# Third and fourth layer steps by image: linear attention, gated mix and the expert combination issued per image in one block

## The reference

```python
# layer 0, feed-forward: one expert of 8 for each token, capacity 128 tokens an expert
x += tanh(g) * gate * (gelu(h @ w1[e]) @ w2[e])          # h = layernorm(x)
# layer 1, attention: linear attention, 16 heads of 8
q = relu((h @ Wq + bq) * 8**-0.5) + 1e-6                 # h = layernorm(x)
k = relu((ctx @ Wk + bk) * 8**-0.5) + 1e-6;  v = ctx @ Wv + bv
x += tanh(g) * ((q @ (k^T v)) / (q . sum(k) + 1e-8) @ Wo + bo)
# layer 1, feed-forward: mix with the token before
xr = mu_r * h + (1 - mu_r) * h_prev;  xk = mu_k * h + (1 - mu_k) * h_prev
x += tanh(g) * (sigmoid(xr @ W_r) * (relu(xk @ W_k)**2 @ W_v))
# layer 2, attention: softmax attention with a mask, 16 heads of 8; then routed experts
```

## Time and profile before

| | |
|---|---|
| runs (us) | 536.28, 536.67, 537.48 |
| profiled execution | 537.36 us, of which the span shown is 535.6 us |
| TensorE (PE) busy | 461.1 us, 86% |
| VectorE (DVE) busy | 293.7 us, 55% |
| ScalarE (ACT) busy | 227.7 us, 43% |
| GpSimd (POOL) busy | 91.1 us, 17% |
| chain that ended last | PE 64%, DVE 21%, ACT 9% |
| granted TensorE clock | 0.964 of full over the span |

### The profile page before, as it was taken

How to read it: one execution, slowest core, us unless ns; L and a number is a source line. 1 busy time by engine, 2 the same in 40 slices (tenths; PEclk the granted TensorE clock), 3 DMA queues, 4 the chain that set the end, 5 groups by cost and what they waited for, 6 DMA issues and landing times.

```text
span 535.6 us, 6990 instructions
## 1 busy us (share of the span) xinstructions
PE 461.1 (86%) x2716; PEld 261.6 (49%) x2716; DVE 293.7 (55%) x577; ACT 227.7 (43%) x442; POOL 91.1 (17%) x77
## 2 busy tenths in 40 slices
PE   5889999988999596888789988889795998997886
PEld 2334433636754233776436754334353465455563
DVE  1666765363225556774254645464898377446661
ACT  4455563303113545453253354535674264425460
POOL 3000000205100002442000000010555505042300
PEclk9999999899998978999799999999998899999799
DMA  8500000800000000000000020000110101101000
GB/s 352 220 2 2 1 1 0 300 2 0 1 1 1 0 0 0 1 2 1 0 2 0 1 78 2 0 2 15 25 21 1 20 1 21 20 2 40 1 0 21
DMA packets 4594, 15.55 MB, mean 29 GB/s; under 512 B 1361, under 2 KB 1618, under 8 KB 4050
## 3 DMA queue, kind: packets, MB, share of 16 engines
q1 hardware_dynamic: 4562, 15.10, 8.6%
HBM read 12.74 MB, written 0.52 MB: 25 GB/s over the span
## 4 chain that ended last, share of the span: by engine, by line
PE 64%; DVE 21%; ACT 9%; issue 3%; DMA 1%; POOL 1%; SPq 0%; DVEq 0%; ACTq 0%
PE PS L484 57%; DVE mxd L2174 3%; ACT wmoe L1602 2%; PE PS L719 2%; ACT xc L1337 1%; PE PS L1153 1%; ACT xc L1339 1%; DVE keys L1898 1%; DVE wmoe L1749 1%; DVE mx L1756 1%; DMA cst<-const_dram 1%; PE PS L555 1%; DVE sw L1702 1%; DVE PS L2167 1%; DVE hp L1693 1%
## 5 line engine op out<-in xcount | busy, mean ns | idle before, releaser
L484 PE MATMUL PS<-PTB,keys 128*64 128x128 f32 (+4 forms) x416 | 46.9, 405 | 0.1
L1602 ACT ACTIVATE wmoe<-PS,mxd 128x512 f32<-128x512 f32 (+3 forms) x64 | 33.0, 525 | 10.3 <-DVE mxd L2174 10.1
L484 PE MATMUL PS<-keys,PTB 32*128 32x231 f32 (+2 forms) x384 | 29.2, 343 | 5.2 <-DVE wmoe L1749 2.7
L2414 POOL TENSOR_TENSOR den<-den,cst 128x1024 f32<-128x1024 f32 x7 | 17.3, 2475 | 86.4 <-DMA den<-wmoe 86.4
L1898 DVE TENSOR_REDUCE keys<-PS 128x9 f32<-128x693 f32 x32 | 26.6, 873 | 9.4 <-PE PS L484 9.4
L484 PEld LDWEIGHTS PS<-PTB,keys 128*64 128x64 f32 (+3 forms) x416 | 22.8, 150 | 16.7 <-issue 13.5
L1614 ACT COPY PTB<-PS 128x768 f32<-128x768 f32 (+1 forms) x24 | 20.8, 867 | 23.6 <-PE PS L1153 23.4
L484 PE MATMUL PS<-x,cst 128*128 128x512 f32 x32 | 20.4, 745 | 11.4 <-DMA cst<-const_dram 6.1
L484 PE MATMUL PS<-wmoe 64*128 64x512 f32 (+3 forms) x128 | 25.0, 490 | 5.9 <-ACT wmoe L1602 5.8
L484 PEld LDWEIGHTS PS<-keys,PTB 32*128 32x128 f32 (+1 forms) x384 | 20.8, 184 | 18.6 <-issue 12.1
L1693 DVE TENSOR_TENSOR hp<-PS,xc 128x512 f32<-128x512 f32 x16 | 11.1, 691 | 33.1 <-ACT xc L1339 33.1
(11 more groups left out here) (348 smaller groups left out, 955.4 us busy)
## 6 DMA issues: line engine op xcount, KB each, us to landing
wmoe<-w_dram SPq DMA_DIRECT2D x2, 2048.0 KB, 12.2
den<-wmoe SPq DMA_DIRECT2D x28, 64.0 KB, 2.3
wa<-wa_dram SPq DMA_DIRECT2D x4, 256.0 KB, 6.3
wlate<-ew_dram SPq DMA_DIRECT2D x2, 512.0 KB, 5.4
wd<-wd_dram SPq DMA_DIRECT2D x1, 1024.0 KB, 8.9
wlate<-wm_dram SPq DMA_DIRECT2D x1, 1024.0 KB, 4.7
cst<-const_dram SPq DMA_DIRECT2D x1, 738.0 KB, 7.6
cst<-const_dram SPq DMA_DIRECT2D x1, 678.0 KB, 4.9
```

The costliest lines, as they stand in the source:

```text
L484: return nc.tensor.matmul(o, l, r, start=start, stop=stop, skip_group_check=True)
L1602: A_(PR[n % 2][:, z, to:to + (t + 1) * 128], PS[:, ring_banks("turn", n).start + z, to:to + (t + 1) * 128], ACT.Exp, bias=mxd[:, n % 2, k, ...
L2414: g.tensor_tensor(turned, turned, table("ropes"), ALU.mult).then_inc(S("d_roped"), 1)
```

## The change

It makes layer 0's combination, linear attention and mix run image by image in one new function `between` on each of the engines.

- The expert loop combines image 0 only (one 128x512 product an expert). Image 1's eight combinations stand in `between`, with VectorE's eight one-hot tiles for them 512 wide. All eight experts' outputs are kept (`eo` has eight tiles).
- Keys, values and their sums of linear attention move into `moe`, between the routing's prefix product and the gather: the keep_clock pair there goes, eight products of 77x128 come, ScalarE makes the features (copy and Relu), GpSimd adds 1e-6, four products of 128 columns sum up, ScalarE copies the sums, GpSimd masks them by head. The gather stands behind these four products on TensorE.
- The denominator is a product of 128x512 with the head sums spread over 128 columns; ScalarE takes Ln and Exp(-1) of it. Reciprocal, widening, transposes and ScalarE's copy of the numerator go.
- The mix is two accumulating products with weights scaled by mu and 1 - mu (GpSimd scales them early), so that VectorE's four mixing steps an image go. The sigmoid is 0.5 (tanh(x/2) + 1); Relu is done by VectorE. Four table loads stand in `between` on ScalarE: for tanh and back, twice.
- Image 1's mix and layernorm 4 stand behind the scores of layer 2's first unit; the three keep_clock products before the unit loop go, and a pair of them is put before the first mix.
- `x_ready`, `ln_h` and the other layernorm semaphores exist once for each image; waits elsewhere keep their meaning.

```diff
+BETWEEN = [("query", 0), ("den", 0), ("num", 0), ("project", 0), ("k", 0), ("query", 1), ("r", 0), ("v", 0),
+           ("den", 1), ("num", 1), ("project", 1), ("k", 1), ("r", 1), ("v", 1)]
+def product(name, b):
+    return BETWEEN.index((name, b)) + 1
...
-        eo = sb("eo", [128, 2, 128])
+        eo = PTB[:, 6:8].rearrange("p a (n d) -> p (a n) d", d=128)
+        GC = [[OT[:, b, n, :] for n in range(2)] for b in range(B)]
...
+        kvs = PTB[:, 2].rearrange("p (n d) -> p n d", d=128)
+        wmix = PTB[:, 3].rearrange("p (n d) -> p n d", d=128)
...
-                keep_clock(0, 512, 512)
+                arrived(pe, "rows", "wa1")
+                for b in range(B):
+                    for j, bias in ((1, "bk1"), (2, "bv1")):
+                        o = PS[0:SK, 6, (j - 1) * 256 + b * 128:(j - 1) * 256 + b * 128 + 128]
+                        mm(o, ctxr[:, b, 0:SK], wa1[:, j, :], stop=False)
+                        last = mm(o, C("ones", 1)[:, 0:SK], R(bias), start=False)
+                last.then_inc(S("lin_kv"), 1)
+                pe.wait_ge(S("lin_kf"), 2)
+                for b in range(B):
+                    mm(PS[:, 6, b * 128:(b + 1) * 128], kf[:, b, :], vs[:, b, :])
+                    last = mm(PS[:, 6, 256 + b * 128:384 + b * 128], kf[:, b, :], C("ones", SK))
+                last.then_inc(S("lin_sum"), 1)
...
-                def combine(e):
-                    pe.wait_ge(S("moe_eo"), e + 1)
-                    pe.wait_ge(S("moe_GT"), e + 1)
-                    for k in range(2):
-                        last = mm(PS[:, 2 + k, :], eo[:, e % 2, :], G[:, e % 2, k * 512:(k + 1) * 512],
-                                  start=(e == 0), stop=(e == E - 1))
-                    last.then_inc(S("moe_combined"), 1)
                 up(0)
                 for e in range(E):
                     if e + 1 < E:
                         up(e + 1)
                     if e >= 1:
-                        combine(e - 1)
+                        combine(e - 1, 0)
                     down(e)
-                combine(E - 1)
...
+            def combine(e, b):
+                pe.wait_ge(S("moe_eo"), e + 1)
+                pe.wait_ge(S("moe_GT"), E * b + e + 1)
+                mm(PS[:, 2 + b, :], eo[:, e, :], GC[b][e % 2], start=(e == 0), stop=(e == E - 1)).then_inc(S("moe_combined"), 1)
+            def between():
+                def lin_query(b):
+                    pe.wait_ge(S(f"ln_h_{b}"), 3)
+                    mm(PS[:, 4 + 2 * b, :], wa1[:, 0, :], h[b]).then_inc(S("between"), 1)
+                def lin_sums(b):
+                    pe.wait_ge(S("lin_kvs"), 2)
                     pe.wait_ge(S("lin_qf"), b + 1)
+                    mm(PS[:, 2 * b + 1, :], kvs[:, 2 + b, :], qf[:, b, :]).then_inc(S("between"), 1)
+                    mm(PS[:, 2 * b, :], kvs[:, b, :], qf[:, b, :]).then_inc(S("between"), 1)
+                def lin_project(b):
                     pe.wait_ge(S("lin_att"), b + 1)
+                    mm(PS[:, 4 + 2 * b, :], wa1[:, 3, :], att[:, b, :]).then_inc(S("between"), 1)
+                def mixed(b, n, bank):
+                    pe.wait_ge(S("wmix"), 4)
+                    pe.wait_ge(S(f"ln_h_{b}"), 4)
+                    mm(PS[:, bank, :], wmix[:, 2 * n, :], h[b], stop=False)
+                    mm(PS[:, bank, :], wmix[:, 2 * n + 1, :], hp[:, b, 0:T], start=False).then_inc(S("between"), 1)
+                def mix_values(b, bank):
+                    pe.wait_ge(S("mix_k2"), b + 1)
+                    mm(PS[:, bank, :], wf1[:, 2, :], att[:, b, :]).then_inc(S("between"), 1)
+                combine(0, 1)
+                combine(1, 1)
+                ln_centre(2, 0)
+                combine(2, 1)
+                ln_variance(2, 0)
+                combine(3, 1)
+                combine(4, 1)
+                lin_query(0)
+                combine(5, 1)
+                lin_sums(0)
+                combine(6, 1)
+                combine(7, 1)
+                lin_project(0)
+                ln_centre(2, 1)
+                ln_centre(3, 0)
+                ln_variance(2, 1)
+                ln_variance(3, 0)
+                keep_clock(5, 512, 512)
                 arrived(pe, "wf1")
+                mixed(0, 1, 4)
+                lin_query(1)
+                mixed(0, 0, 0)
+                mix_values(0, 1)
+                lin_sums(1)
+                ln_centre(4, 0)
+                lin_project(1)
+                ln_variance(4, 0)
+                pe.wait_ge(S("at_k_placed"), 1)
+                query2(0, 0, 4)
+                query2(0, 1, 5)
+                ln_centre(3, 1)
+                scores2(0, (0, 1))
+                ln_variance(3, 1)
+                scores2(0, (2, 3))
+                mixed(1, 1, 6)
+                mixed(1, 0, 7)
+                mix_values(1, 4)
+                ln_centre(4, 1)
+                ln_variance(4, 1)
+                query2(1, 0, 4)
+                query2(1, 1, 5)
...
+                act.wait_ge(S("lin_kv"), 1)
+                nc.scalar.copy(vs[:], PS[0:SK, 6, 256:512].rearrange("p (b f) -> p b f", b=B))
+                A_(kf[:], PS[0:SK, 6, 0:256].rearrange("p (b f) -> p b f", b=B), ACT.Relu, scale=8 ** -0.5).then_inc(S("lin_kf"), 1)
                 act.preload_act_table_set(GELUS)
-                context(1, "bk2", ACT.Identity, "bo2")
+                act.wait_ge(S("lin_sum"), 1)
+                nc.scalar.copy(kvs, PS[:, 6, :].rearrange("p (n f) -> p n f", n=2 * B)).then_inc(S("lin_kvs"), 1)
...
+            def between():
+                def lin_shares(b):
+                    act.wait_ge(S("between"), product("den", b))
+                    link(A_(xc[:, b, :], PS[:, 2 * b + 1, :], ACT.Ln, bias=C("tiny")))
+                    A_(xc[:, b, :], xc[:, b, :], ACT.Exp, scale=-1.0).then_inc(S("lin_rec"), 1)
+                def lin_project(b):
+                    act.wait_ge(S("between"), product("project", b))
+                    A_(yb[:, b, :], PS[:, 4 + 2 * b, :], ACT.Identity, bias=V("bo1")).then_inc(S("lin_y"), 1)
+                def mix_gate(b, bank):
+                    act.wait_ge(S("between"), product("r", b))
+                    A_(PTB[:, 4 + b, :], PS[:, bank, :], ACT.Tanh, scale=0.5).then_inc(S("mix_gate"), 1)
+                norm(2, 0)
+                lin_shares(0)
+                lin_project(0)
+                ln_squares(2, 1)
+                ln_squares(3, 0)
+                ln_root(3, 0)
+                ln_root(2, 1)
+                act.preload_act_table_set(TANHS)
+                mix_gate(0, 0)
                 act.preload_act_table_set(ROOTS)
+                lin_shares(1)
+                ln_squares(4, 0)
+                ln_root(4, 0)
+                lin_project(1)
+                place2(0, 0, 4)
+                place2(0, 1, 5)
+                ln_squares(3, 1)
+                ln_root(3, 1)
+                act.preload_act_table_set(TANHS)
+                weights2(0, 0)
+                weights2(0, 1)
+                mix_gate(1, 7)
+                weights2(0, 2)
+                weights2(0, 3)
+                ln_squares(4, 1)
+                act.preload_act_table_set(ROOTS)
+                ln_root(4, 1)
+                place2(1, 0, 4)
+                place2(1, 1, 5)
...
+                    place_tokens(e, 0)
                     dve.wait_ge(S("moe_down"), e + 1)
+                    v.tensor_copy(eo[:, e, :], PS[:, 6 + e % 2, 0:128]).then_inc(S("moe_eo"), 1)
+            def place_tokens(e, b):
+                if e >= 2:
+                    dve.wait_ge(S("moe_combined"), E * b + e - 1)
+                v.tensor_scalar(GC[b][e % 2], destb[:, b * T:(b + 1) * T], C("slotid")[:, e:e + 1], None,
+                                ALU.is_equal).then_inc(S("moe_GT"), 1)
+            def between():
+                def moe_add(b):
+                    dve.wait_ge(S("moe_combined"), E * (b + 1))
                     link(v.tensor_tensor(yb[:, b, :], gateb[:, b * T:(b + 1) * T], PS[:, 2 + b, :], ALU.mult))
                     residual(b, 4)
+                def lin_features(b):
+                    dve.wait_ge(S("between"), product("query", b))
+                    link(v.tensor_scalar(qf[:, b, :], PS[:, 4 + 2 * b, :], V("bq1"), 8 ** -0.5, ALU.add, ALU.mult))
                     v.tensor_scalar(qf[:, b, :], qf[:, b, :], 0.0, 1e-6, ALU.max, ALU.add).then_inc(S("lin_qf"), 1)
+                def lin_divide(b):
+                    dve.wait_ge(S("lin_rec"), b + 1)
+                    dve.wait_ge(S("between"), product("num", b))
+                    v.tensor_tensor(att[:, b, :], PS[:, 2 * b, :], xc[:, b, :], ALU.mult).then_inc(S("lin_att"), 1)
+                def lin_add(b):
                     dve.wait_ge(S("lin_y"), b + 1)
                     residual(b, 1)
+                def mix_square(b, bank):
+                    dve.wait_ge(S("between"), product("k", b))
+                    link(v.tensor_scalar(att[:, b, :], PS[:, bank, :], 0.0, None, ALU.max))
```

(98 more changed lines are left out.)

270 lines of the change are left out of this document (72 added, 198 removed).

## The result

Median 541.87 us against 536.67 before; ratio 1.0089, 95% interval 1.0066 to 1.0112, over 11 runs of each. The profiled execution takes 541.38 us with a span of 539.3, against 537.36 and 535.6. The forecast was 535.5, "faster" the likeliest sign; the time lies above the range's end of 538.6.

A forecast was written before the change was run, and what follows sets the result against it. TensorE's queue bounds the expert loop; after it, a chain of single tiles with waiting. A full-clock gain of 7.9, less 4.2 in front and 2.5 late clock, leaves 1.2 us: 535.5 against 536.67, range 532.0 to 538.6.

The forecast's parts named there:

- Expert loop: Loop over experts: seven halves of combinations leave it, so image 0's last combine starts at 151.2 instead of 157.23 us.
- The stage at full clock: Image 0's last combine to `turn_keys`: 56.5 us at full clock, `turn_keys` starting at 207.7 instead of 215.57.
- the schedule: Step-by-step walk of four engine queues at full-clock prices from the last combine to `turn_keys`, giving a gain of 7.9 us.
- Wait ahead of the gather: Before the expert gather: new products, ScalarE and GpSimd steps make it 2.6 us late, bounds 2.2 and 3.0.
- Clock in the front: Four sums and first gather tile run partly at half clock: cost 1.6 us, between 0 and 2.6.
- Late clock: Stage after the last combine: two falls to half clock likely, costing 2.5 us, bounds 0 and 5.2.
- the slower rival: Half clock through image 1's tail, second scores to last queries: costs 5.3 us, time 538.3; chance 0.30.
- The sum: Whole kernel: 7.9 gained, less 4.2 in front and 2.5 late clock, 1.2 us faster.
- The 7.9 us: Gain at full clock up to `turn_keys`, measured against a start of 215.57 that includes the stage's old clock loss.
- Table loads: ScalarE in `between`: two of four loads on the path, 1.28 us each; rival doubles that, 538.1 us, chance 0.08.

The follow-up runs named there:

- e1: Changed kernel plus nine TensorE products on constants in the late stage's idle places, none in the front: ratio 0.9980, 536.58 us.
- e4: Changed kernel with the four sums behind the second gather tile and nine products on constants in the late stage: ratio 0.9881, 530.78 us; same code again 0.9931.
- e2: Changed kernel plus two products on constants in TensorE's wait ahead of the four sums and the gather: ratio 1.0018, 537.46 us.
- e8: Changed kernel plus five products on constants, around image 1's last centre, variance and queries only: ratio 1.0030, 537.69 us.
- e6: Changed kernel plus four products on constants, before image 0's last queries and before the second scores only: ratio 1.0059, 540.29 us.
- e11: The changed kernel itself, unaltered, measured once more on another set of runs: ratio 1.0099, 541.01 us.
- e3: Changed kernel with the four sums and their wait moved behind the second gather tile: ratio 0.9985, 537.16 us.
- e9: Changed kernel without GpSimd's step adding 1e-6 to the key features, TensorE waiting for ScalarE alone: ratio 1.0065, 540.03 us.
- e5: Kernel before the change plus products on constants, four ahead of the mix and two between layer 2's first and second scores: ratio 0.9966, 535.36 us.
- e7: Changed kernel with later sums and nine late products on constants, without the four table loads, Tanh replaced by Identity: ratio 0.9925, 532.60 us.

## Why the prediction was wrong, point by point

- **Expert loop: right.** 6.0 us predicted, 6.01 measured.
- **The stage at full clock: right to 1 us.** 56.5 us by the schedule, 57.50 in e1 and e4. The added products hold at most 0.1 of the difference. 0.45 of it stands at one step: VectorE's residual of image 1's mix took 1.20 us, in the changed kernel (206.93) and in e1, where the schedule had 0.75. GpSimd's subtraction ran beside it (206.37, 1.22 us); no run shows whether that is the reason. Read as distances from the last combine (151.2 in the schedule, 157.09 here, so 5.9 later) its milestones were met as long as the clock was full: x of image 0 ready at 159.7 (153.8 predicted), layernorm 2 at 164.8 (158.9), layernorm 3 at 178.5 (172.45), x again at 185.6 (179.45), layernorm 4 at 191.4 (185.1). The scores, behind the half clock from 193, start at 195.55 where the schedule had 193.8; x of image 1 at 208.1 where it had 205.7; the last layernorm ends at 214.2 instead of 210.8.
- **Wait ahead of the gather: right in kind, a little small.** 2.87 us (e2) for 2.6; GpSimd's step took 0.86 where I had taken 0.7.
- **Clock in the front: mis-sized for this execution.** I took 1.6 of a possible 2.6; it was 2.61, the upper bound. The four sums and most of the first two gather tiles ran at half clock. The front took 13.26 - 7.78 = 5.48 more, where the sum has 4.2. But e1 and e8 have the same front and took 12.31: there the clock cost 12.31 - 10.65 = 1.66, as forecast. So 1.6 was within what this front does, and 2.61 too (changed kernel, e6, e11).
- **Late clock: the step that failed.** I wrote "Two falls of the length seen from 186 to 192 or less are likely", worth 2.5. The stage was 62.20 - 56.5 = 5.7 us over the schedule: 4.7 of it clock, shown by e1, and 1.0 the schedule's. The second fall lasted 10.2 us, longer than the one of the earlier trace rows. The other profiles without products in the tail lie over 2.5 too: stages of 60.74 (e2, e6), 61.11 (e11), 62.28 (e3) and 62.22 us (e9), 3.2 to 4.8 over 57.50. The mark set for it, a stage of more than 61 us, was passed. What happened is the slower rival's place and mechanism: nothing in the tail brought the clock up before the unit loop. Its list was too long for this execution, though (the half clock began only at the variance product; in e11 it also lay on k and r), and its price of 5.3 was not reached even with the earlier fall: 3.2 and 1.5 make 4.7.
- **The sum.** 7.9 - 5.5 - 5.7 = -3.3, against +1.2 forecast and -3.7 in the spans (0.39 of which arose ahead of all this).
- **Why the chances were off.** The 7.9 us were stated as including the old clock loss in the stage. e5 shows that loss: 4.6 us. So some 3.3 of the 7.9 was order (measured 2.3, by e4 against e5, the schedule being 1.0 short), and the rest was a clock that the new stage had to hold although TensorE has much to wait for in it (busy 7.93 of the 13.6 us before the last fall). I counted the 4.6 as won and then charged only 2.5 for the new stage, with no row that said it would do better than the old. The rows gave a bound for it: 0.12 of 56.4 us lost to the clock, 6.8 us at most. In hindsight, pricing the new stage's clock like the old one's, 4.6, and the front's at its upper bound gives 7.9 - 5.2 - 4.6 = -1.9, the right sign.
- **Table loads: out** as a rival. The sum took them at their row and put two on the path; they cost less still, since TensorE's products run beside them. After the load at 183.88 ScalarE's next instruction begins at 185.17, 0.01 us after its end. The Trainium skill, "ScalarE: Activation LUTs", section "What ACT_TABLE_LOAD costs", has a drain of 1380 ns behind the load; this trace shows none. e7 finds 0.3 us for four loads together.

What stays open: when the clock falls and for how long differs between executions of the same instructions (in the front 6.8 us in the changed kernel, e6 and e11, 3.4 in e1 and e8; before the second scores a fall in the changed kernel and none in e2), and no run here says what sets it. So a clock term read from a single profile is uncertain by about 1 us in the front and 1.5 us in the stage (60.74 to 62.28 us over the five profiles whose stage is the changed kernel's: its own, e2, e3, e9, e11).

## What to carry to other kernels

When an order of work at full clock is compared with a profiled stage, take the profiled stage's half-clock time out first; what the new order gains beyond that must be paid for by keeping TensorE busy. Put new work with a wait behind the next long piece of the queue, not ahead of it: four sums moved behind the second gather tile took 5.3 us off the front. And fill waits on TensorE that its clock depends on: nine products on constants, 7.7 us of work that no one needs, made the stage 4.7 us shorter. Price such a clock term as a range over several profiles: one may show a fall that the next one lacks.

## What the hardware did that I had not expected

- The clock fell with TensorE little idle: in the front it was busy 10.02 of 12 us before 111.0, with the products of 77x128 from 107.15 to 110.14 and then 0.86 us of idle time.
- A fall is not short: 6.8 us in the front, 10.2 in the tail; 3.4 us was the shortest in these stretches, and the tail stayed at half while the two queries kept TensorE busy for 3.78 us on end.
- GpSimd took 0.86 us for a scalar step on 77x256, between the 0.61 that it took on 128x128 (at 112.34 in the changed kernel) and the 1.06 on 128x308.
